# Sparsemax attention of a two-layer decoder: five loops written out, waits for constants moved to their instructions

## The chip, the cores and the metric

The kernel runs as one program on one core of a Trainium2 chip. The core has five engines with an instruction stream each: TensorE (PE, with its weight loads PEld), VectorE (DVE), ScalarE (ACT), GpSimd (POOL) and SyncE (SP), which here only starts transfers. They meet through semaphores: an instruction adds to one when it is done, and another instruction, or a separate waiting instruction in front of it, holds until the semaphore has reached a value. The metric is the device time of one execution in microseconds (us), the median of several runs.

## The reference

A decoder of two layers over 32 sequences of 100 rows of 256 numbers, in float32. Each layer has self attention, cross attention to a context of 361 rows, and a feed-forward block, each with a residual and a layer norm. The diff touches the cross attention of the second layer, whose weights come from a sparsemax in place of a softmax:

```python
def sparsemax(x):
    x = x - jnp.max(x, axis=-1, keepdims=True)
    zs = -jnp.sort(-x, axis=-1)
    rho = jnp.arange(1, L + 1, dtype=x.dtype)
    cssv = jnp.cumsum(zs, axis=-1) - 1.0
    support = zs > cssv / rho
    k = jnp.maximum(jnp.sum(support, axis=-1, keepdims=True), 1)
    tau = jnp.take_along_axis(cssv, k - 1, axis=-1) / k.astype(x.dtype)
    return jnp.clip(x - tau, 0.0)
scores = einsum('bhqd,bhkd->bhqk', qh, kh) * scale     # 16 heads of 16
out = einsum('bhqk,bhkd->bhqd', sparsemax(scores), vh) # then @ Wo + bo, residual, layer norm
```

## The kernel before

Seven stages follow each other, each with its own semaphores and tiles, whose names begin with the stage: `ta` (tanh attention), `ca` (cross attention), `ql` (quantised linear), `na` (normed attention), `sa` (the sparsemax attention), `me` and `ea` (experts), `cr` (collecting their rows). Between `sa` and `me` stands a second sparsemax stage `sb` behind a condition that these inputs do not meet, so it does not run. In each stage every engine has a program of its own; the order on each engine is the order in which its Python code calls the instructions, and nothing reorders it.

`sa` (`packed_sparse_attention`) handles one sequence at a time. Its 16 heads x 100 query rows are 1600 score rows, packed into 13 tiles of up to 128 rows x 361 keys, in two groups of 7 and 6 tiles. For a group the work runs around the engines. PE multiplies the scores (`scores`, L2747 and L2751), ACT copies them out of PSUM (`copy_scores`, L2882), and DVE takes the eight largest of each eighth of a row (`largest`, eight MAX8 at L3036 for each tile). From these candidates DVE and POOL work out a lower bound of the threshold: `bound` (L3052, L3055), then twice a `compare` on POOL (L2631) and a `refine` on DVE (L3065 to L3078, each instruction working on 6 or 7 columns that the one before it wrote), and L3085 to L3089 end it with `nt0`. With `nt0` ACT cuts the scores (`cut`, L2890), DVE counts what is left (`number`, L3098), DVE makes a Newton step (`update`, L3119 to L3130), ACT sums the excess (`excess`, `sign`, L2898 and L2906), DVE makes a second Newton step, and POOL subtracts the threshold (`probability`, L2641). PE turns the result (`turn`, L2765), ACT copies it (L2916), and PE multiplies by the values (`values`) and the output matrix.

The two groups are staggered, so that DVE goes through one sequence in two halves, each beginning with the `update` at L3119 and ending with the `nt0` at L3089 of the other group. Call half A the one that ends with group 0 of the next sequence (7 tiles), half B the one that ends with group 1 (6 tiles).

`passes` (L2595 to L2605) drives PE, ACT, DVE and POOL: `body` is written out for the first two sequences (m = 0), stands in a hardware loop for the next 28, two to a turn (`eng.Fori(1, B // 2 - 1)`, 14 turns), and is written out again for the last two and for what remains behind them. SP has a loop of its own (L2581, 13 turns). In a loop the values that semaphores are compared with come from a register that is worked out at run time; in the written-out parts they are constants.

`stand` (L91 to L96) is how several waits are put: a wait, and then an increment of a semaphore `turns` that nobody reads. The wait is carried by the increment, which is an instruction of its own in front of the one that needs the value. `Chain` uses it between DVE instructions that read each other's results, and between POOL's. Other waits are put with `wait_ge` alone, and then ride on the instruction that needs them, in the loop with a register's value as well as outside with a constant.

Of the kernel before, what the change touches and what calls it, by code (L numbers as in the profile page):

```python
# [26 lines left out]
B = 32  # L27
# [35 lines left out]
def open_all(eng, *events):  # L63

    for e in events:
        eng.sem_inc(e.sem, e.start)


class Chain:
# [15 lines left out]
    def wait(self):  # L85
        stand(self.eng, self.turns, self.sem, self.i * self.per + self.n)
# [5 lines left out]
def stand(eng, turns, sem, value):  # L92


    eng.wait_ge(sem, value)
    eng.sem_inc(turns, 1)  # L96


class Place:
# [53 lines left out]
def tanh_attention(nc, x, xT, Wq, bq, Wk, bk, Wv, bv, Wo, bo, out):  # L153
# [8 lines left out]
    with ExitStack() as ctx:  # L162
# [107 lines left out]
        def _(pool):  # L270
# [6 lines left out]
            with pool.Fori(0, G) as g:  # L277
                chain = Chain(pool, turns, pool_step, g, U * NORM_STEPS)

                def causal(u):  # L280

                    for r in range(4):
                        stand(pool, turns, *exp_done.at(g, 4 * u + r + 1))
                        heads = pT[:, u % 2, 4 * r:4 * r + 4, :]
                        pool.affine_select(out=heads, in_=heads, compare_op=ALU.is_ge, fill=0.0, base=0,  # L285
                                           pattern=[[0, 4], [1, S]], channel_multiplier=-1).then_inc(p_done.sem, 1)

                def norm(u):

                    pool.wait_ge(*stored[u % 2].at(g, u // 2))  # L290
                    stand(pool, turns, *mv_done.at(g, u + 1))
                    norm_rows(pool, chain, z[:, u % 2, :], mv[:, u % 2, :], rstd[:, u % 2, :], nbias[:, u % 2, :],
                              half[0:S, :], xn[:, u % 2, :], xn_done.sem)

                causal(0)
                causal(1)
                causal(2)
                norm(0)
                causal(3)
                norm(1)  # L300
                norm(2)
                norm(3)
                chain.end()
# [2064 lines left out]
def packed_sparse_attention(nc, x, cT, heads4, Wq, bq, Wk, bk, Wv, bv, WoS, bo, out, sum_max):  # L2368
# [20 lines left out]
    with ExitStack() as ctx:  # L2389
# [60 lines left out]
        turns = a.sem("turns")  # L2450
# [53 lines left out]
        def prev(m, u):  # L2504
            return (m, 0) if u else (m - 1, 1)
# [22 lines left out]
        @block.sync  # L2528
        def _(sp):
            open_all(sp, *xq_in, *cT_in, *xr_in, *stored)  # L2530
            sp.dma_start(wq[:, :, :], Wq.rearrange("(k p) n -> p k n", p=P)).then_inc(w_in, 16)
            sp.dma_start(wk[:, :, :], Wk.rearrange("(k p) n -> p k n", p=P)).then_inc(w_in, 16)
            sp.dma_start(wv[:, :, :], Wv.rearrange("(k p) n -> p k n", p=P)).then_inc(w_in, 16)
            sp.dma_start(wo[:, :, :], WoS.rearrange("(k p) n -> p k n", p=P)).then_inc(w_in, 16)
            sp.dma_start(bos[:, :], bo).then_inc(w_in, 16)
            sp.dma_start(bqs[:, :], bq).then_inc(w_in, 16)
            sp.dma_start(bks[:, :], bk).then_inc(w_in, 16)
            sp.dma_start(bvs[:, :], bv).then_inc(w_in, 16)
            sp.dma_start(hm[:, :], heads4).then_inc(w_in, 16)

            def load_x(m, u):
                n = 2 * m + u
                sp.wait_ge(*proj_done.at(n, -7))
                sp.dma_start(xq[:, u, :], x_s[n]).then_inc(xq_in[u].sem, 16)

            def load_c(m, u):
                n = 2 * m + u
                sp.wait_ge(*vp_done.at(n, -3))
                sp.dma_start(cTs[:, u, :, :], cT_s[n]).then_inc(cT_in[u].sem, 16)

            def load_residual(m, u):
                n = 2 * m + u
                sp.wait_ge(*xb_done.at(n, -1))
                sp.dma_start(xr[:, u, :], x_s[n]).then_inc(xr_in[u].sem, 16)

            def store(m, u):
                n = 2 * m + u
                sp.wait_ge(*xn_done.at(n, 1))
                sp.dma_start(out_s[n], xn[:, u, :]).then_inc(stored[u].sem, 16)

            def step(m, u, third=True, second=True, stores=True):

                if third:
                    load_x(m + 1 + u, 1 - u)
                if second:
                    load_c(m + 1, u)
                    load_residual(m + 1, u)
                if stores:
                    store(*prev(m, u))

            last = B // 2 - 1
            load_x(0, 0)
            load_c(0, 0)
            load_x(0, 1)
            load_c(0, 1)
            load_residual(0, 0)
            load_residual(0, 1)
            load_x(1, 0)
            step(0, 0, stores=False)
            step(0, 1)  # L2580
            with sp.Fori(1, last - 1) as m:  # L2581
                step(m, 0)
                step(m, 1)
            step(last - 1, 0)
            step(last - 1, 1, third=False)
            step(last, 0, third=False, second=False)
            step(last, 1, third=False, second=False)
            store(last, 1)
            sp.wait_ge(top_step, 1)
            sp.dma_start(sum_max, top[:, :]).then_inc(top_out, 16)  # L2590
            for u in range(2):
                sp.wait_ge(*stored[u].at(B // 2, 0))
            sp.wait_ge(top_out, 16)

        def passes(eng, body):  # L2595

            body(0, 0, behind=False)
            body(0, 1)
            with eng.Fori(1, B // 2 - 1) as m:
                body(m, 0)  # L2600
                body(m, 1)
            body(B // 2 - 1, 0, later=False)
            body(B // 2 - 1, 1, ahead=False, later=False)
            body(B // 2, 0, here=False, ahead=False, later=False)

        @block.gpsimd
        def _(pool):
# [75 lines left out]
            compare(0, 0, 0, 0)  # L2683
            compare(0, 0, 0, 1)
            passes(pool, sequence)

        @block.tensor
        def _(pe):
# [158 lines left out]
            for i in range(10):  # L2847
                scores(0, 0, i)
            passes(pe, sequence)

        @block.scalar
        def _(act):
# [56 lines left out]
            def copy_turned(m, u, q, t):  # L2909
                n = 2 * m + u  # L2910
                f = NK * q + t
                kn = KEYS[t][1]
                _, c0, cn = quad(q)
                act.wait_ge(*ov_done.at(n, 0))
                act.wait_ge(*tr_done.at(n, f + 1))
                act.activation(pT[0:kn, t, c0:c0 + cn], tr[f % 2][0:kn, 0:cn], ACT.Relu).then_inc(ca_done.sem, 1)  # L2916
# [85 lines left out]
            for i in range(7):  # L3002
                copy_scores(0, 0, i)
            passes(act, sequence)

        @block.vector
# [1105 lines left out]
```

## Time and profile before

| | |
|---|---|
| time, 3 runs | 4163.66 us median (4158.6 to 4169.7) |
| profiled execution, span | 4163.3 us, 83513 instructions |
| busy in the span | PE 3203.5 (77%), DVE 2250.9 (54%), ACT 2196.6 (53%), POOL 1452.4 (35%) |
| stage `sa` in the span | about 2130 to 3470 us |

The profile gives no separate time for the profiled execution; its span, first to last instruction, stands for it and lies 0.4 us under the median of the runs. Busy shares of the whole span mix seven stages with different limits, so the stage is read by itself. In a row of the timeline the two numbers ahead are the start and the duration in us, and a bracket at the end gives idle time of the engine in front of the instruction and what ended it, "issue" being time for which the profile shows no cause. Idle times of up to about 0.2 us get no bracket; they are the difference between a start and the end of the row before.

### The profile page before, as it was taken

The numbers are of one execution on the slowest core, as the hardware profiler recorded it, in microseconds if no ns is written. First come the engines' busy times: TensorE is split into PE (matmuls) and PEld (weight loads), VectorE is DVE, ScalarE is ACT, GpSimd is POOL, SyncE is SP. The second block draws the span as 40 slices with busy tenths as digits, with TensorE's granted clock in tenths as the row PEclk, the third lists the DMA queues.
The fourth block names the chain that finished last, engine by engine and source line by source line (L and its number), as shares of the span: only waits on it lengthen the run. The fifth ranks groups of instructions, "written<-read, shape, count | busy, mean of one in ns | idle before, by whom it ended". The sixth has DMA issues, their size and how long they took to land. (4 is left out here: it accounts for less than half of the span.)

```text
span 4163.3 us, 83513 instructions
## 1 busy us (share of the span) xinstructions
PE 3203.5 (77%) x21166; PEld 1978.6 (48%) x21166; DVE 2250.9 (54%) x10359; ACT 2196.6 (53%) x6653; POOL 1452.4 (35%) x2228
## 2 busy tenths in 40 slices
PE   7999998888888823888857777777777785687772
PEld 5666665566666622444424444444444444344441
DVE  1222222466666675666648888878887882211112
ACT  3433333466666601777738777777777782221110
POOL 1111111355555535555524444444443441110005
PEclk9999999899999966888858888887888775999996
DMA  1000000111111011000010000000000003206773
GB/s 61 20 12 12 14 14 10 56 37 38 36 37 35 26 38 48 21 22 22 21 39 15 18 17 17 20 16 18 16 18 16 18 8 128 77 31 207 225 228 110
DMA packets 111885, 189.45 MB, mean 46 GB/s; under 512 B 11150, under 2 KB 95886, under 8 KB 105550
## 3 DMA queue, kind: packets, MB, share of 16 engines
q1 hardware_dynamic: 102094, 166.32, 12.9%
q10 hardware_dynamic: 7200, 14.68, 0.9%
q0 software_dynamic: 2400, 6.56, 0.5%
q14 instruction: 151, 1.24, 0.1%
q8 instruction: 40, 0.66, 0.1%
HBM read 149.90 MB, written 37.62 MB: 45 GB/s over the span
## 5 line engine op out<-in xcount | busy, mean ns | idle before, releaser
L3036 DVE MAX8 sa_cand<-sa_s 128x8 f32<-128x45 f32 (+3 forms) x3328 | 405.6, 191 | 37.1 <-ACT sa_s L2882 30.9
L2765 PE MATMUL sa_tr<-sa_ident,sa_s 128*128 128x128 f32 (+3 forms) x1248 | 276.5, 339 | 187.5 <-POOL sa_s L2641 100.2
L852 ACT ACTIVATE ca_p<-ca_sm,ca_nb 100x361 f32<-100x361 f32 x512 | 301.9, 591 | 210.9 <-DVE ca_nb L936 209.9
L672 POOL TENSOR_SCALAR ca_p<-ca_p,ca_rec 100x361 f32<-100x361 f32 x512 | 286.8, 579 | 344.2 <-DVE ca_rec L950 343.9
L2641 POOL TENSOR_SCALAR sa_s<-sa_s,sa_unit,sa_nu 128x361 f32<-128x361 f32 (+1 forms) x416 | 261.4, 644 | 317.5 <-DVE sa_nu L3128 317.5
L2765 PEld LDWEIGHTS sa_tr<-sa_ident,sa_s 128*128 128x128 f32 (+3 forms) x1248 | 185.9, 179 | 284.9 <-issue 274.4
L2890 ACT ACTIVATE sa_s<-sa_s,sa_nt 128x361 f32<-128x361 f32 (+1 forms) x416 | 244.3, 592 | 94.1 <-DVE sa_nt L3089 94.1
L936 DVE CUSTOM_DVE_ANT_0 ca_sm<-ca_sc,ca_mb 100x361 f32<-100x361 f32 x512 | 252.3, 526 | 69.3 <-PE ca_sc L759 56.4
L2898 ACT ACTIVATE sa_spare_a<-sa_s,sa_nu 128x361 bf16<-128x361 f32 (+1 forms) x416 | 246.8, 594 | 69.5 <-DVE sa_nu L3130 69.3
L2631 POOL TENSOR_TENSOR sa_over<-sa_cand,sa_tc 128x280 f32<-128x280 f32 (+3 forms) x128 | 99.3, 776 | 453.2 <-DVE sa_tc L3055 277.6
L2751 PE MATMUL sa_sc<-sa_kT,sa_qm 32*128 32x361 f32 (+3 forms) x768 | 227.9, 522 | 20.5 <-ACT sa_s L2882 20.0
L2916 ACT ACTIVATE sa_pT<-sa_tr 128x512 f32<-128x512 f32 (+5 forms) x384 | 181.7, 497 | 103.6 <-PE sa_tr L2765 100.7
L770 PEld LDWEIGHTS ca_tr<-ca_ident,ca_p 100*128 100x128 f32 (+1 forms) x1536 | 171.9, 154 | 102.3 <-issue 73.5
L770 PE MATMUL ca_tr<-ca_ident,ca_p 100*128 100x100 f32 (+1 forms) x1536 | 208.8, 260 | 3.2 <-POOL ca_p L672 2.5
L3098 DVE TENSOR_SCALAR_CACHE_REDUCE sa_spare_d<-sa_s 128x361 bf16<-128x361 f32 (+1 forms) x416 | 202.9, 518 | 0.3 <-ACT sa_s L2890 0.3
L1628 ACT ACTIVATE na_p<-na_sm,na_nb 100x100 f32<-100x100 f32 x512 | 186.6, 370 | 22.3 <-DVE na_nb L1693 20.6
L2730 PE MATMUL sa_yo<-sa_wv,sa_cTs 128*128 128x256 f32 (+1 forms) x384 | 155.2, 544 | 50.8 <-DVE sa_vm L3025 50.7
L465 DVE TENSOR_TENSOR ta_vpre<-ta_proj,ta_bvs 100x512 f32<-100x512 f32 x64 | 44.3, 692 | 276.2 <-PE ta_proj L337 276.2
L2882 ACT ACTIVATE sa_s<-sa_sc 128x361 f32<-128x361 f32 (+1 forms) x416 | 178.1, 463 | 18.7 <-PE sa_sc L2751 14.2
L285 POOL TENSOR_SCALAR_AFFINE_SELECT ta_pT<-ta_pT 100x400 f32<-100x400 f32 x128 | 67.9, 542 | 318.6 <-ACT ta_pT L428 314.3
L1457 POOL TENSOR_TENSOR na_rs<-na_rs,na_half 100x32 f32<-100x32 f32 x32 | 174.5, 5453 | 2.7
L2751 PEld LDWEIGHTS sa_sc<-sa_kT,sa_qm 32*128 32x128 f32 (+3 forms) x768 | 83.1, 183 | 155.5 <-ACT sa_s L2882 92.6
(323 smaller groups left out, 7683.4 us busy)
## 6 DMA issues: line engine op xcount, KB each, us to landing
ea_we<-m_experts SPq DMA_DIRECT2D x40, 1024.0 KB, 6.4
ea_wd<-m_experts SPq DMA_DIRECT2D x40, 512.0 KB
ca_cTs<-cT SPq DMA_DIRECT2D x32, 361.0 KB
sa_cTs<-cT SPq DMA_DIRECT2D x32, 361.0 KB
rows_in<-me_zeros ACTq DMA_DIRECT2D x1, 7168.0 KB
ea_xe<-rows_in SPq DMA_DIRECT2D x40, 128.0 KB
rows_out<-ea_ye ACTq DMA_DIRECT2D x40, 128.0 KB
ca_ms<-mask SPq DMA_DIRECT2D x32, 141.0 KB
```

The lines of the kernel that those rows point to most:

```text
L672: ins = pool.tensor_scalar(p[:, r, j, :], p[:, r, j, :], rec[:, r, j:j + 1], 1.0, ALU.mult, ALU.mult)
L770: mm = pe.transpose(tr[f % 2][0:kn, j * S:(j + 1) * S], p[:, r, j, k0:k0 + kn], ident[0:S, 0:S])
L852: act.activation(p[:, r, j, :], sm[:, r % 2, j, :], ACT.Exp, bias=nb[:, r % 2, j:j + 1], scale=-1.0, accum_out=den[:, r, j:j + 1]).then_in ...
L936: dve.tensor_tensor_reduce(sm[:, r % 2, j, :], sc[j][0:S, 0:S2], mb[:, u, :], -1 / 4, 3e38, ALU.add, ALU.min, nb[:, r % 2, j:j + 1]).then_ ...
L1628: act.activation(p[:, r, j, :], sm[:, r, j, :], ACT.Exp, bias=nb[:, r, j:j + 1], scale=-1.0, accum_out=den[:, r, j:j + 1]).then_inc(exp_do ...
L2641: pool.tensor_scalar(s[0:rows, u, i, :], s[0:rows, u, i, :], unit[0:rows, :], nu2[0:rows, i:i + 1], ALU.mult, ALU.add).then_inc(p_done.sem, 1)
L2751: mm = pe.matmul(bank[0:rows, 0:S2], qm[hr, u, P * i:P * i + rows], kT[hr, u, i // 7, :], start=True, stop=True)
L2765: mm = pe.transpose(tr[f % 2][0:kn, c0:c0 + rows], s[0:rows, u, i, k0:k0 + kn], ident[0:rows, 0:rows])
L2890: act.activation(s[0:rows, u, i, :], s[0:rows, u, i, :], ACT.Relu, bias=nt0[0:rows, i:i + 1], accum_out=total[0:rows, i:i + 1]).then_inc(r ...
L2898: ins = act.activation(spare_a[0:rows, i, :], s[0:rows, u, i, :], ACT.Relu, bias=nu1[0:rows, i:i + 1], accum_out=total[0:rows, i:i + 1])
L3036: ins = dve.max(cand[0:rows, i, q, :], s[0:rows, u, i, PART[q]:PART[q + 1]])
L3098: ins = dve.tensor_scalar(spare_d[0:rows, i, :], s[0:rows, u, i, :], u1[0:rows, i:i + 1] if step else 0.0, 0.0, ALU.is_gt, ALU.add, accum_ ...
```

## The change

`stand` adds its increment only where the value is not a plain integer. Where it is one, the wait now rides on the next instruction of the engine. And the two loops of `sa`, in `passes` for four engines and in SP's program, become Python loops, so all 32 sequences are written out and every value in the stage is a constant.

```diff
     eng.wait_ge(sem, value)
-    eng.sem_inc(turns, 1)
+    if not isinstance(value, int):
+        eng.sem_inc(turns, 1)
@@ SP's program of packed_sparse_attention
-            with sp.Fori(1, last - 1) as m:
+            for m in range(1, last - 1):
                 step(m, 0)
                 step(m, 1)
@@ passes, for PE, ACT, DVE and POOL
-            with eng.Fori(1, B // 2 - 1) as m:
+            for m in range(1, B // 2 - 1):
                 body(m, 0)
                 body(m, 1)
```

Line numbers from 97 on are one higher after the change. The program of DVE in this stage goes from 1539 instructions (559 ahead of the loop, 591 in it, 389 behind it) to one run of 5907; those of PE from 1011 to 4232, of ACT from 547 to 2602, of POOL from 274 to 878. The order of the computing instructions on every engine is the same as before. The edit of `stand` touches the written-out parts of other stages too: outside `sa` and `sb`, 131 waits with a constant stood as instructions of their own on DVE and 114 on POOL, nearly all of which now ride on the instruction behind them.

On DVE, the end of the loop's second half A and the beginning of the next half B, before (instructions that only wait are not shown; REGISTER_ALU works out the value for one):

```order
L95 REGISTER_ALU
L3078 TENSOR_TENSOR sa_tc<-sa_tc,sa_shift 128x7
L95 REGISTER_ALU
L3085 TENSOR_SCALAR sa_low<-sa_tc 128x7
L3086 TENSOR_SCALAR sa_low<-sa_tc 128x7
L95 REGISTER_ALU
L3089 TENSOR_TENSOR sa_nt<-sa_low 128x7
L2599 REGISTER_ALU
L2599 COMPARE_AND_BRANCH
```

The same place on DVE after the change, the end of a half (here one with 6 columns) and the start of the next:

```order
L3079 TENSOR_TENSOR sa_tc<-sa_tc,sa_shift 128x6
L3086 TENSOR_SCALAR sa_low<-sa_tc 128x6
L3087 TENSOR_SCALAR sa_low<-sa_tc 128x6
L3090 TENSOR_TENSOR sa_nt<-sa_low 128x6
L3120 TENSOR_SCALAR sa_count<-sa_signs 128x4
L3121 RECIPROCAL sa_rec<-sa_count 128x7
L3037 MAX sa_cand<-sa_s 128x8 x4
```

The branch and the register work are gone, and the next half follows directly; the computing rows stand in the order in which they stood.

On POOL, in the loop before, the two `compare` of group 0 and what follows them:

```order
L95 ISA
L2631 TENSOR_TENSOR sa_over<-sa_cand,sa_tc 128x7x40
L95 REGISTER_ALU
L2631 TENSOR_TENSOR sa_over<-sa_cand,sa_tc 128x7x64
L2653 REGISTER_ALU
L143 TENSOR_SCALAR sa_rstd<-sa_mv 100x1
```

The same place on POOL after the change:

```order
L2632 TENSOR_TENSOR sa_over<-sa_cand,sa_tc 128x7x40
L2632 TENSOR_TENSOR sa_over<-sa_cand,sa_tc 128x7x64
L144 TENSOR_SCALAR sa_rstd<-sa_mv 100x1
```

Here too only the instructions between the computing ones went; each `compare` now carries its own wait for `tc`.

## Rows read from the trace of the kernel before

**Rows 1.** Busy time by engine, 28 sequences of the loop (window: length, then each engine).

```profile
2214.50:3363.00 1148.50, 893.12 (x5686) 515.41 (x5684) 950.18 (x5460) 897.97 (x2772) 472.31 (x700) 0.81 0.06 17
```

**Rows 2.** What DVE waited for, 2100 to 3500: us in total, times, longest.

```profile
DVE sa_count L3119 <- issue: 51.9, 14, 4.2
DVE sa_over L3065 <- POOL sa_over L2631: 51.4, 98, 1.1
...
DVE sa_cand L3036 <- issue: 3.6, 14, 0.3
...
DVE sa_spare_d L3098 <- ACT sa_s L2890: 0.3, 1, 0.3
```

**Rows 3.** Timeline of DVE: starts of halves in the loop and behind it.

```profile
2704.16 0.17 DVE L3119 TENSOR_SCALAR sa_count<-sa_signs 128x4 f32<-128x4 f32 x1
...
2727.98 0.17 DVE L3119 TENSOR_SCALAR sa_count<-sa_signs 128x4 f32<-128x4 f32 x1 [4.06 <-issue]
...
2747.50 0.17 DVE L3119 TENSOR_SCALAR sa_count<-sa_signs 128x4 f32<-128x4 f32 x1
...
2767.30 0.17 DVE L3119 TENSOR_SCALAR sa_count<-sa_signs 128x4 f32<-128x4 f32 x1
...
3363.15 0.17 DVE L3119 TENSOR_SCALAR sa_count<-sa_signs 128x4 f32<-128x4 f32 x1
...
3383.02 0.17 DVE L3119 TENSOR_SCALAR sa_count<-sa_signs 128x4 f32<-128x4 f32 x1
...
3402.21 0.17 DVE L3119 TENSOR_SCALAR sa_count<-sa_signs 128x4 f32<-128x4 f32 x1
...
3421.57 0.17 DVE L3119 TENSOR_SCALAR sa_count<-sa_signs 128x4 f32<-128x4 f32 x1
```

**Rows 4.** Groups by line, DVE: count | busy us, mean ns | idle before us.

```profile
L3069 DVE TENSOR_REDUCE sa_both<-sa_over 128x14 f32<-128x560 f32 (+3 forms) x128 | 109.7, 857 | 18.7
L3072 DVE RECIPROCAL sa_few<-sa_both 128x6 f32<-128x6 f32 (+1 forms) x128 | 25.3, 197 | 19.0 <-DVE sa_both L3069 0.5
L3120 DVE RECIPROCAL sa_rec<-sa_count 128x6 f32<-128x6 f32 (+1 forms) x128 | 25.2, 197 | 12.1 <-DVE sa_count L3119 2.3
L3075 DVE SCALAR_TENSOR_TENSOR sa_shift<-sa_both,sa_few 128x6 f32<-128x6 f32 (+1 forms) x128 | 24.9, 195 | 9.4
L3078 DVE TENSOR_TENSOR sa_tc<-sa_tc,sa_shift 128x6 f32<-128x6 f32 (+1 forms) x128 | 21.4, 167 | 18.8
L3142 DVE BATCH_NORM_STATS2 sa_stats<-sa_z 100x6 f32<-100x256 f32 x32 | 13.7, 427 | 1.1
L3085 DVE TENSOR_SCALAR sa_low<-sa_tc 128x7 f32<-128x7 f32 x64 | 11.0, 172 | 9.5
L3089 DVE TENSOR_TENSOR sa_nt<-sa_low 128x7 f32<-128x7 f32 x64 | 10.7, 167 | 12.4 <-DVE sa_low L3086 5.1
```

**Rows 5.** Timeline of DVE and POOL in one half A: DVE's `tc`, POOL's `compare`, DVE's answer.

```profile
2762.24 0.17 DVE L3078 TENSOR_TENSOR sa_tc<-sa_tc,sa_shift 128x7 f32<-128x7 f32 x1
...
2762.58 0.94 POOL L2631 TENSOR_TENSOR sa_over<-sa_cand,sa_tc 128x448 f32<-128x448 f32 x1 [2.97 <-DVE sa_tc L3078]
...
2763.55 0.43 DVE L3065 TENSOR_SCALAR sa_over<-sa_over 128x448 f32<-128x448 f32 x1 [0.65 <-POOL sa_over L2631]
```

**Rows 6.** Groups by line, POOL: a separate wait (L144) and one on its instruction (L1457).

```profile
L1457 POOL TENSOR_TENSOR na_rs<-na_rs,na_half 100x32 f32<-100x32 f32 x32 | 174.5, 5453 | 2.7
L144 POOL TENSOR_TENSOR sa_rstd<-sa_rstd,sa_half 100x1 f32<-100x1 f32 x32 | 18.3, 571 | 5.9 <-POOL sa_rstd L143 5.9
```

**Rows 7.** Timeline of ACT in one sequence: its four waits for DVE.

```profile
2756.42 0.59 ACT L2898 ACTIVATE sa_spare_a<-sa_s,sa_nu 128x361 bf16<-128x361 f32 x1 [1.60 <-DVE sa_nu L3130]
...
2767.39 0.60 ACT L2890 ACTIVATE sa_s<-sa_s,sa_nt 128x361 f32<-128x361 f32 x1 [1.53 <-DVE sa_nt L3089]
...
2776.45 0.60 ACT L2898 ACTIVATE sa_spare_a<-sa_s,sa_nu 128x361 bf16<-128x361 f32 x1 [1.18 <-DVE sa_nu L3130]
...
2786.70 0.60 ACT L2890 ACTIVATE sa_s<-sa_s,sa_nt 128x361 f32<-128x361 f32 x1 [1.88 <-DVE sa_nt L3089]
```

## The prediction

> **What bounds the stage now.** I read the busy shares by stage first, then what VectorE (DVE) waited for, then its timeline, and last the idle time in front of each of its lines. In the loop's 28 sequences DVE is busy 950.2 of 1148.5 us, more than PE (893.1) and ACT (898.0) [rows 1]. That alone proves little, since PE and ACT are close behind. The list of DVE's waits decides it: in the whole stage it waited 0.3 us for an ACT result inside the stream of tiles, and its two large rows name neither ACT nor PE [rows 2]. Its 198.3 idle us therefore have other owners. 51.9 us stand in front of L3119 with no cause shown, 51.4 us are waits for POOL's `compare` [rows 2], and the rest are short idle times in front of lines that read what DVE itself has just written [rows 4]. DVE sets the pace here: time that leaves its stream leaves the kernel, until another engine becomes late.
>
> **The loop's end.** A half A that runs into the loop's jump back takes 2727.98 - 2704.16 = 23.82 us; the next half A, inside the turn, takes 2767.30 - 2747.50 = 19.80 [rows 3]. The last half A of the loop, which leaves it without a jump, takes 3383.02 - 3363.15 = 19.87, with no pause in front of the L3119 that follows [rows 3]. So the pause belongs to the jump that is taken, 13 times in 14 turns: 13 x 4.02 = 52.3 us. Written out, DVE's code has no jump between the first sequence and the last. I take 52. During the pause the other engines drain and wait, so none of it comes back as somebody else's delay.
>
> **The waits between DVE's own instructions.** L3072 (a reciprocal behind a reduction) has 19.0 us of idle for 128, 148 ns each; L3069 and L3078 read the same, 146 and 147 [rows 4]. In front of each stands a separate waiting instruction. L3142 reads the row just written as well, but its wait rides on it: 1.1 us for 32, 34 ns each [rows 4]. L3120 has both kinds, 64 each, and its 12.1 us fit 64 x 147 + 64 x 34 ns = 11.6 [rows 4]. Exposed separate waits: L3069, L3072, L3075, L3078 and L3085 have 18.7 + 19.0 + 9.4 + 18.8 + 9.5 = 75.4 us; L3089 64 x 147 ns = 9.4 (the other 3.0 of its 12.4 belong to the loop's end, counted above); L3120 9.9; two lines outside the rows, L3052 and L3144, 32 waits each and priced like the others, 9.4. Together 104 us, or 22 waits for each of 32 sequences. Each now rides on its instruction: 104 x (1 - 34/147) = 80 us less. Bounds: 0, if the idle time belongs to the dependency and not to the extra instruction, and 104. I take 80, because the 34 ns stand in the same stream and between instructions of the same kind. Separate waits that are already met cost nothing I can see: the MAX8 behind them start without a gap.
>
> The Trainium skill, VectorE: DVE Perf Modes, section "The DRAIN you can't avoid", speaks against this term: it reports eight copies taking the same time with a semaphore on each as with one on the last, so that the semaphore costs nothing extra. By that rule this term would be 0 and the time that of rival 2 below. It measured increments, though; what goes here is an instruction that waits, and rows 4 price that at 113 ns.
>
> **POOL's answer.** Four times a sequence DVE hands `tc` to POOL and, after at most one other instruction, waits for `compare`; 98 of 128 waits show [rows 2], three a sequence. In one of them `tc` is done at 2762.24 + 0.17 = 2762.41, POOL starts at 2762.58, and DVE goes on 0.03 us after POOL ends [rows 5]. Of these 0.17 us the separate wait is some 0.10: POOL's L144 behind such a wait has 5.9 us for 32, 184 ns, and its L1457 with the wait riding on it 2.7 for 32, 84 ns [rows 6]. 98 x 0.10 = 9.8 us; bounds 0 and 98 x 0.17 = 16.7. I take 10.
>
> **Register work.** In the loop DVE also works out a register for nearly every wait. Behind the loop, in written-out code, half B takes 3402.21 - 3383.02 = 19.19 us against 2747.50 - 2727.98 = 19.52 inside, and half A 3421.57 - 3402.21 = 19.36 against 19.80 [rows 3]. That is at most 0.33 + 0.44 = 0.77 us a sequence, 28 x 0.77 = 21.6 us. It includes the loop's one pause a turn in front of L3036, 3.6 us in all [rows 2], and perhaps help from PE and ACT, which have less to do there. Bounds 0 and 21.6; I take 9, a little under the middle.
>
> **What rides elsewhere.** The 131 DVE and 114 POOL waits that change outside this stage would give 131 x 0.113 + 114 x 0.10 = 26 us if all were exposed, 0 if all hide. In those stages other engines set the pace for most of the time; I take 3.
>
> **What is late next.** ACT. In one undisturbed sequence, half A of 19.80 us [rows 3] and half B of 2786.70 - 2767.39 = 19.31 [rows 7], it waits for DVE 1.60, 1.53, 1.18 and 1.88 us [rows 7], 6.2 in all, so of 39.1 us it needs 32.9. DVE goes from the same 39.1 to about 39.1 - 22 x 0.113 - 0.3 for POOL - 0.3 for the registers = 36.0 us: still the longer. Phase by phase it is tight in one place: between the Newton step and `nt0` of half A, DVE loses 12 of the 22 waits and one POOL answer, 12 x 0.113 + 0.10 = 1.46 us, against 1.53 of slack. ACT then starts at once instead of waiting, which delays nobody as long as it catches up in the next phase, where it has 1.18.
>
> **Sum.** 52 + 80 + 10 + 9 + 3 = 154 us. The profiled execution spans 4163.3 us, 0.4 under the median of the runs; against that median the changed kernel takes 4163.7 - 154 = 4010 us.
>
> **Rivals.**
> 1. ACT or PE takes over. If half of what DVE gains outside the loop's end comes back as waits for ACT's cuts or PE's scores, 52 + 99 / 2 = 102 us are left: 4062. For it: ACT's slack is as small as 1.18 us [rows 7]. Against: DVE has waited 0.3 us for it in a stage where ACT's slack never vanished, and 32.9 stands against 36.0.
> 2. The 147 ns belong to the dependency, and a wait at its instruction costs as much. Then POOL's answer is unchanged as well, and 52 + 9 + 3 = 64 us are gained: 4100. Against it: L3142 and L1457 [rows 4, 6]. The Trainium skill's sentence above (VectorE: DVE Perf Modes) speaks for this one.
> 3. The straight code runs dry, and it is slower. 5907 instructions come past once where 591 came round; should fetching them pause DVE as the jump does, 4.0 us each time, then 154 / 4.0 = 38 pauses cancel the gain, one in 155 instructions, and 42 make it measurably slower (4180). The closing code, 389 instructions without a jump, and the opening code, 559, show no such pause: the 14 pauses at L3119 [rows 2] are 13 jumps and one at the loop's entry. By the 0.26 us pauses at L3036, one for 591 instructions, it would be 10 x 0.26 = 2.6 us, less than the 3.6 that go. The Trainium skill, Runtime: NRT & Kernel Launch, section "Instruction fetch mechanics", has code arrive in blocks of 256 instructions, with the crossing mostly hidden; as an estimate from that page, 5907 / 256 = 23 crossings, fewer than the 38 even if each cost a whole jump.
> 4. The change does not do what it says: the increments come back as other waiting instructions. The program has 236 of these left on DVE in this stage against 133 + 14 x 100 + 98 executed before, so this has next to no chance.
>
> **How the numbers follow.** The forecast's mechanism has 0.75, rival 1 0.11, rival 2 0.08, rival 3 0.06 in all: 0.03 for slower, 0.01 for no change, 0.02 for a smaller gain. Within 0.3% (12.5 us) a measurement of this kernel can't tell a difference from none. Faster 0.96, same 0.01, slower 0.03. The range goes down to 3990: POOL's answer at 16.7, register work at 21.6, and nothing else at its end, give 3991. Upwards it takes in rival 1 and most of the way to rival 2, to 4085; what lies above has about 0.1.
>
> **What would show it.** In the profile after, the pause at L3119 (now L3120) is gone and the halves lie 17.6 to 18.3 us apart throughout; the idle in front of the lines of rows 4 falls to about 4 us for 128; POOL starts `compare` 0.07 us after `tc`; ACT's waits for `nt0` shrink from 1.5 to 1.9 us to under 0.8. Wrong would be: the same 147 ns in front of L3073 (rival 2), DVE waiting for ACT or PE by more than 10 us in the stage (rival 1), or new pauses without a cause spread evenly over DVE or PE (rival 3).

## The result and the profile after

The changed kernel takes 3969.97 us, median of 4 runs (3966.1 to 3982.3), against 4166.51 (4158.6 to 4169.7) for the kernel before, run beside it: ratio 0.954, 95% interval 0.952 to 0.956. The forecast was 4010, its range 3990 to 4085. The direction was right, and what was forecast to go went; but the gain is 196 us by the medians and 193.1 by the two profiled spans (4163.3 and 3970.2), where 154 was forecast, and the time lies below the range.

The length of the stage can be read from one line: the distance between the first and the last start of the `update` instruction (L3119 before, L3120 after). Before it is 3454.0 - 2176.1 = 1277.9 us. The view of one line of the kernel after has count, duration in ns (least, median, most) and first and last start:

```profile
L3120 DVE TENSOR_SCALAR sa_count<-sa_signs x64: 167/170/171, 2162.8 to 3266.7; 128x4 f32<-128x4 f32 x64
```

That is 1103.9 us. So 174.0 of the 193.1 us come from the stage and 19.1 from outside it, 13.3 of these ahead of it (2176.1 to 2162.8). The 19.1 rest on one profile of each kernel, and the part outside the stage varies by more than 10 us between profiles of kernels that are alike there (shown with the other stages below). I use the length of the stage for every experiment below; it depends less than the whole time on what the other stages happen to do.

The busy times in the windows of the kernel after, for the 28 sequences that had been the loop (columns as in [rows 1]):

```profile
2198.00:3183.30 985.30, 812.01 (x5684) 481.50 (x5684) 926.05 (x5461) 886.59 (x2772) 473.20 (x700) 0.89 0.07 20
```

1148.5 us have become 985.3. DVE is now busy 94% of the time and still longest. PE needs 812.0 us where it needed 893.1 for the same number of matmuls: its granted clock rose from 0.81 to 0.89. So one of the two engines that rival 1 feared got faster as well.

Of the 163.2 us in this window, 139.1 are idle time of DVE (198.3 before, 59.3 after). The other 24.1 are busy time (950.2 before, 926.1 after) for the same instructions: more often now the next one starts while the one before is still running, and some run a little shorter. The clearest place is a MAX8 behind a reciprocal, before and after:

```profile
2747.82 0.20 DVE L3120 RECIPROCAL sa_rec<-sa_count 128x7 f32<-128x7 f32 x1
2748.06 0.53 DVE L3036 MAX8 sa_cand<-sa_s 128x8 f32<-128x45 f32 x4
```

```profile
2761.25 0.20 DVE L3121 RECIPROCAL sa_rec<-sa_count 128x7 f32<-128x7 f32 x1
2761.37 0.48 DVE L3037 MAX8 sa_cand<-sa_s 128x8 f32<-128x45 f32 x4
```

From start to start it was 0.24 us, without a gap that a bracket would show; now it is 0.12, and the two overlap by 0.08 us.

What DVE waited for in the kernel after (us in all, times, longest):

```profile
DVE sa_over L3066 <- POOL sa_over L2632: 41.6, 98, 1.0
...
DVE sa_count L3120 <- ACT sa_spare_a L2899: 5.7, 1, 5.7
...
DVE sa_count L3120 <- issue: 0.3, 1, 0.3
```

The 51.9 us in front of `update` are gone, and the wait for POOL fell from 51.4 to 41.6 [rows 2]. The single wait for ACT stands at the end of the stage. The halves in DVE's timeline now follow each other without a pause (start, duration):

```profile
2708.16 0.17 DVE L3120 TENSOR_SCALAR sa_count<-sa_signs 128x4 f32<-128x4 f32 x1
...
2725.88 0.17 DVE L3120 TENSOR_SCALAR sa_count<-sa_signs 128x4 f32<-128x4 f32 x1
...
2743.32 0.17 DVE L3120 TENSOR_SCALAR sa_count<-sa_signs 128x4 f32<-128x4 f32 x1
...
2761.05 0.17 DVE L3120 TENSOR_SCALAR sa_count<-sa_signs 128x4 f32<-128x4 f32 x1
```

17.72 us for half B, 17.44 for half A; [rows 3] had 19.52, 19.80 and 23.82. The prediction had said 17.6 to 18.3, so half A is shorter than forecast. The groups by line that answer to [rows 4]:

```profile
L3070 DVE TENSOR_REDUCE sa_both<-sa_over 128x14 f32<-128x560 f32 (+3 forms) x128 | 109.7, 857 | 4.4
L3073 DVE RECIPROCAL sa_few<-sa_both 128x6 f32<-128x6 f32 (+1 forms) x128 | 25.2, 197 | 4.4
L3121 DVE RECIPROCAL sa_rec<-sa_count 128x6 f32<-128x6 f32 (+1 forms) x128 | 25.2, 197 | 4.6 <-DVE sa_count L3120 0.2
L3079 DVE TENSOR_TENSOR sa_tc<-sa_tc,sa_shift 128x6 f32<-128x6 f32 (+1 forms) x128 | 21.4, 167 | 4.4
L3143 DVE BATCH_NORM_STATS2 sa_stats<-sa_z 100x6 f32<-100x256 f32 x32 | 13.7, 427 | 1.1
```

The last column is the one to read: 18.7 to 19.0 us for 128 have become 4.4, 34 ns each, the value that L3142 had before. The mean durations of these lines did not change. The 0.34 us between `tc` and POOL's start [rows 5] became 0.24 in the timeline after:

```profile
2774.29 0.17 DVE L3079 TENSOR_TENSOR sa_tc<-sa_tc,sa_shift 128x7 f32<-128x7 f32 x1
...
2774.53 0.94 POOL L2632 TENSOR_TENSOR sa_over<-sa_cand,sa_tc 128x448 f32<-128x448 f32 x1 [2.21 <-DVE sa_tc L3079]
...
2775.50 0.43 DVE L3066 TENSOR_SCALAR sa_over<-sa_over 128x448 f32<-128x448 f32 x1 [0.55 <-POOL sa_over L2632]
```

ACT's waits in one sequence: 0.70 and 0.70 us where [rows 7] had 1.88 and 1.60, and 1.25 where it had 1.18. The one in front of the first `cut` of the group of seven tiles, 1.53 before, is now too short for a bracket:

```profile
2761.17 0.60 ACT L2891 ACTIVATE sa_s<-sa_s,sa_nt 128x361 f32<-128x361 f32 x1 [0.70 <-DVE sa_nt L3090]
...
2769.33 0.59 ACT L2899 ACTIVATE sa_spare_a<-sa_s,sa_nu 128x361 bf16<-128x361 f32 x1 [0.70 <-DVE sa_nu L3131]
...
2787.28 0.60 ACT L2899 ACTIVATE sa_spare_a<-sa_s,sa_nu 128x361 bf16<-128x361 f32 x1 [1.25 <-DVE sa_nu L3131]
```

### The profile page after: what moved, and what is told of

Same layout as the page of the kernel before. It is cut to its first block and busy times, and to the rows that moved or that the text cites. A ratio compares the mean times of both kernels' runs of the same rounds, so it can differ in the third digit from the quotient of the medians.

```text
span 3970.2 us, 76439 instructions
## 1 busy us (share of the span) xinstructions
PE 3117.0 (79%) x21166; PEld 1942.5 (49%) x21166; DVE 2225.5 (56%) x10359; ACT 2184.4 (55%) x6653; POOL 1452.7 (37%) x2228
## 3 DMA queue, kind: packets, MB, share of 16 engines
q1 hardware_dynamic: 102094, 166.32, 13.3%
## 5 line engine op out<-in xcount | busy, mean ns | idle before, releaser
L2766 PE MATMUL sa_tr<-sa_ident,sa_s 128*128 128x128 f32 (+3 forms) x1248 | 231.1, 306 | 111.7 <-ACT sa_pT L2917 96.8
L937 DVE CUSTOM_DVE_ANT_0 ca_sm<-ca_sc,ca_mb 100x361 f32<-100x361 f32 x512 | 252.3, 526 | 69.7 <-PE ca_sc L760 65.9
L2899 ACT ACTIVATE sa_spare_a<-sa_s,sa_nu 128x361 bf16<-128x361 f32 (+1 forms) x416 | 247.3, 595 | 56.9 <-DVE sa_nu L3131 56.7
L2766 PEld LDWEIGHTS sa_tr<-sa_ident,sa_s 128*128 128x128 f32 (+3 forms) x1248 | 165.8, 161 | 180.8 <-ACT sa_pT L2917 126.1
```

The costliest lines, as they stand in the source:

```text
L937: dve.tensor_tensor_reduce(sm[:, r % 2, j, :], sc[j][0:S, 0:S2], mb[:, u, :], -1 / 4, 3e38, ALU.add, ALU.min, nb[:, r % 2, j:j + 1]).then_ ...
L2766: mm = pe.transpose(tr[f % 2][0:kn, c0:c0 + rows], s[0:rows, u, i, k0:k0 + kn], ident[0:rows, 0:rows])
L2899: ins = act.activation(spare_a[0:rows, i, :], s[0:rows, u, i, :], ACT.Relu, bias=nu1[0:rows, i:i + 1], accum_out=total[0:rows, i:i + 1])
```

## Experiments

Two groups of questions: which edit brings what (the first five), and where the 40 us more than forecast come from (the others). My theory was that two terms were too small: separate waits that are already met, which I had priced at nothing, would cost something behind a short instruction, and the other stages' waits were not hidden. The rivals to that are the prediction's own terms. "Separate again" below means that the named waits get their increment back, with everything else as in the changed kernel:

```diff
+def alone(eng, turns, sem, value):
+    eng.wait_ge(sem, value)
+    eng.sem_inc(turns, 1)
```

**One edit without the other.** First, `stand` alone, the loops kept (in the diff of the change, only the first part).

> Only the edit of stand; the two loops stay, so the 28 sequences inside keep their increments, and only the 4 written-out sequences and the other stages change. The prediction's terms: 4 x 22 x 0.113 = 10 us, POOL 1, elsewhere 3, together 14 us: ratio to before 0.9966. Rival (from the trace after the change: separate waits that are already met also cost something behind a short instruction, and the other stages gained about 19 us): 4 x 3.4 + 19 = 33 us, ratio 0.992. If the other stages' 19 us come from elsewhere than the waits, ratio 0.9966 too.

4127.6 us, ratio 0.992 (0.990 to 0.993), 36 us less. The stage is 16.7 us shorter. By the starts of the halves, 9.9 of these come from the written-out sequences (the three halves ahead of the loop and the four behind it take 118.9 us where they took 128.8), where 11 were forecast. Some 6.6 come from the loop, in which no DVE instruction was changed: the pause at its jump is 3.3 to 3.6 us here and not 3.9 to 4.2, as the wait list shows against [rows 2]:

```profile
DVE sa_count L3120 <- issue: 45.1, 14, 3.6
```

Why the same loop pauses for less behind a shorter opening is open. The span falls by 36.5 us, so 19.8 us come from outside the stage in these two profiles, as my theory had it.

Second, the loops alone, every increment kept.

> Only the loops written out; stand keeps its increment for every value. The prediction's terms: 52 for the loop's end and 9 for register work, 61 us, ratio 0.985. Rival: the register work is worth its upper bound, 0.77 us a sequence, 52 + 22 = 74 us, ratio 0.982. If straight code ran dry it would show pauses without a cause on DVE and a ratio above 0.99. Idle in front of the lines that read what DVE has just written stays at 146 to 148 ns each in all accounts.

4103.2 us, ratio 0.985 (0.984 to 0.987), 61 us less. That is the sum the prediction gave, but partly by luck: the stage is 1209.3 us long, 68.6 shorter, and what lies outside it came out 7 us longer in this profile than in that of the kernel before. The 68.6 are the 51.9 of the pauses and 16.7 of what the prediction calls register work. The groups by line show the separate waits at their old price, 154 ns each here:

```profile
L3072 DVE RECIPROCAL sa_few<-sa_both 128x6 f32<-128x6 f32 (+1 forms) x128 | 25.2, 197 | 19.7 <-DVE sa_both L3069 1.5
```

The timeline of DVE in this kernel shows something new. Most halves take 19.15 to 19.20 us, but some take 0.3 more:

```profile
3007.27 0.17 DVE L3119 TENSOR_SCALAR sa_count<-sa_signs 128x4 f32<-128x4 f32 x1
...
3026.45 0.17 DVE L3119 TENSOR_SCALAR sa_count<-sa_signs 128x4 f32<-128x4 f32 x1
...
3045.96 0.17 DVE L3119 TENSOR_SCALAR sa_count<-sa_signs 128x4 f32<-128x4 f32 x1
...
3065.51 0.17 DVE L3119 TENSOR_SCALAR sa_count<-sa_signs 128x4 f32<-128x4 f32 x1
```

19.18, 19.51, 19.55. 23 of 58 halves are late by more than 0.1 us, about 7 us in all; in the changed kernel it is 2 of 59, 0.7 us. These irregular delays have no owner in the profile. They look like a mild form of rival 3, but that they are instruction fetch I have not shown. They are not chance, though: in the next run, which has the same DVE program in the stage, the same 23 halves are late.

**Whose jump.** In the kernel before, only DVE's loop is written out, or only those of the other engines (there SP's too); increments stay.

```diff
-            with eng.Fori(1, B // 2 - 1) as m:
-                body(m, 0)
-                body(m, 1)
+            if loop:
+                with eng.Fori(1, B // 2 - 1) as m:
+                    body(m, 0)
+                    body(m, 1)
+            else:
+                for m in range(1, B // 2 - 1):
+                    body(m, 0)
+                    body(m, 1)
```

> The kernel before with DVE's loop alone written out; PE, ACT, POOL and SP keep theirs, and every increment stays. If the jump that counts is DVE's: as much as with all loops written out, 69 us in the stage, ratio to before 0.984. Rival: the other engines jump too and their slack is only 1.2 to 1.9 us a half; if their jumps take 4 us as well and were hidden only behind DVE's, then 2 to 3 us a turn come back, 13 x 2.5 = 32 us, ratio 0.991, with DVE waiting for ACT or PE once a turn.

> The kernel before with the loops of PE, ACT, POOL and SP written out; DVE keeps its own, and every increment stays. If the jump and the register work that count are DVE's: ratio to before 0.999 to 1.000, the pauses in front of L3119 still 13 x 4.0 us. Rival: the others' jumps are part of the pause: up to 20 us less, ratio 0.995.

DVE's loop alone: 4095.9 us, ratio 0.984 (0.981 to 0.986), stage 1209.4 us, the same as with all loops written out (1209.3). The others' loops alone: 4169.7 us, ratio 1.002 (1.000 to 1.003), stage 1278.9. What DVE waited for in that kernel:

```profile
DVE sa_count L3124 <- issue: 51.7, 14, 4.1
```

The pause and the register work are DVE's own. The other engines jump too, but what that costs them is hidden even when DVE no longer jumps. With the increments in place, writing out the other four loops brought nothing. POOL's has a use all the same: `stand` drops the increment only for a constant, so the 9 to 13 us of POOL's waits below need POOL's loop written out too.

**A jump for four sequences instead of two.** On PE, ACT, DVE and POOL, in the kernel before.

```diff
-            with eng.Fori(1, B // 2 - 1) as m:
-                body(m, 0)
-                body(m, 1)
+            with eng.Fori(0, (B // 2 - 2) // 2) as k:
+                for m in (2 * k + 1, 2 * k + 2):
+                    body(m, 0)
+                    body(m, 1)
```

> The kernel before with four sequences to a turn instead of two (7 turns, 6 jumps in place of 13) on PE, ACT, DVE and POOL; increments and registers stay. If the pause is paid once for each jump taken: 7 x 4.02 = 28 us less, ratio 0.993. If it grows with the code that comes round again: 0, ratio 1.000, with 6 pauses of about 8 us.

4129.2 us, ratio 0.992 (0.990 to 0.994). The wait list names 21.1 us in front of L3120, 7 times, where 51.9 stood [rows 2]; six of them are jumps of 3.1 to 4.0 us, as this one in the timeline:

```profile
2706.39 0.17 DVE L3120 TENSOR_SCALAR sa_count<-sa_signs 128x4 f32<-128x4 f32 x1 [3.99 <-issue]
```

The pause is paid per jump and does not grow with a body twice as long. The stage is 36.4 us shorter; 30.8 of these are the pauses, and 1.8 the short pause in front of the MAX8, 3.6 us before [rows 2] and 1.8, 7 times, here. The remaining 3.8 I have not assigned. All register instructions are still there, so not all of what the loop costs beside its jumps is register work.

**The exposed waits.** The six waits of `refine` separate again (20 a sequence).

> The changed kernel, but the six chain waits of each refine step on DVE are separate instructions again (20 a sequence, 640 in all, of which 18 a sequence stand behind the instruction whose result they wait for, and 2 behind a copy, where they are met already). The prediction: 18 x 32 x 0.113 = 65 us over the changed kernel, near 4035, ratio to before 0.969. If the time belongs to the dependency and not to the separate instruction: 0, 3970, ratio 0.953. If the met waits cost about 0.1 us too: 65 + 6 = 71 us, ratio 0.970.

4036.2 us, ratio 0.971 (0.969 to 0.974), 66 us over the changed kernel. The stage is 1168.6 us, 64.7 more; forecast was 65. In the groups by line the reciprocal behind the reduction has its 148 ns back, while the one in `update`, whose wait was left riding, keeps 36 ns:

```profile
L3079 DVE RECIPROCAL sa_few<-sa_both 128x6 f32<-128x6 f32 (+1 forms) x128 | 25.2, 197 | 19.0 <-DVE sa_both L3076 0.5
L3127 DVE RECIPROCAL sa_rec<-sa_count 128x6 f32<-128x6 f32 (+1 forms) x128 | 25.2, 197 | 4.6 <-DVE sa_count L3126 0.2
```

Same dependency, same instruction, and the time follows the separate instruction. Rival 2 is refuted.

**The waits that are met already.** In front of the MAX8 groups, first the three right behind a reciprocal, then the other ten; the condition of the second is the reverse.

```diff
-                    stand(dve, turns, *z_in.at(n, pos + 1))
+                    (alone if pos in (0, 7, 11) else stand)(dve, turns, *z_in.at(n, pos + 1))
```

> The changed kernel, but in front of three of the thirteen MAX8 groups of a sequence, those right behind a reciprocal of 0.17 us, the wait for ACT's copy is a separate instruction again (96 in all, already met). The prediction's view, that met waits cost nothing: 0, ratio to before 0.953. Rival: a separate instruction behind a short one keeps the next from starting while the short one ends, 0.09 to 0.14 us each: 96 x 0.12 = 11 us, ratio 0.9555, and the MAX8 start 0.1 us later behind the reciprocal.

> The changed kernel, but the wait in front of the other ten MAX8 groups of a sequence, which stand behind longer work or behind other MAX8, is a separate instruction again (320 in all, already met). The prediction's view: 0, ratio to before 0.953. Rival that only short neighbours matter: 0 to 3 us as well. Rival that every instruction taken costs its own time whatever stands in front: 320 x 0.11 = 35 us, ratio 0.961.

Behind a reciprocal: 3976.2 us, ratio 0.955 (0.953 to 0.957); the stage is 1106.5 us, 2.6 more. The others: 3966.0 us, ratio 0.954 (0.952 to 0.955), stage 1103.8, nothing. Then the rest of DVE's waits in the stage, those of `bound`, `update` and `output`, separate again. These are 16 a sequence (the expectation counts 14): four exposed, twelve met.

> The changed kernel with the remaining DVE waits of this stage (in bound, update and output: 14 a sequence, 448 in all) as separate instructions again; refine and the MAX8 keep theirs at the instruction. Four a sequence stand exposed behind the instruction whose result they read. The prediction: 4 x 32 x 0.113 = 14 us over the changed kernel, the other ten nothing; stage length from the first to the last L3119 near 1118 us. Rival: the met ones cost 0.03 to 0.06 us each as well (the runs so far leave 17 us of the stage unassigned): 14 + 10 x 32 x 0.05 = 30 us, stage 1134.

3996.6 us, ratio 0.960 (0.958 to 0.962). The stage is 1120.4 us, 16.5 more: the four exposed ones at their 0.11 us, and 2.5 for the twelve, about what irregular delays make in this kernel (8 or 9 of 59 halves late, 2 us). So my theory on the met waits fell: for constants the prediction's sentence that they cost nothing holds, but for the 2.6 us behind a reciprocal.

**POOL's answer.** The wait of `compare` separate again.

> The changed kernel, but POOL's wait in front of each compare is a separate instruction again (128). The prediction's term: 98 waits of DVE longer by 0.10 us each: 10 us, ratio to before 0.9555; DVE's waits for compare go from 41.6 back to 51.4 us. Rival that POOL's wait costs the same either way: 0, ratio 0.953.

3980.6 us, ratio 0.956 (0.955 to 0.958). DVE's wait list has the old number to the tenth [rows 2], and the stage is 1113.0 us, 9.1 more:

```profile
DVE sa_over L3072 <- POOL sa_over L2638: 51.4, 98, 1.1
```

**All together.** With groups put back one by one, 93 us of the 105.4 between the loops-only kernel (1209.3) and the changed one (1103.9) were accounted for: 64.7 + 16.5 + 2.6 + 9.1. So all of DVE's waits in the stage separate again, and all of POOL's.

> The changed kernel with every DVE wait of this kind in the stage as a separate instruction again; POOL's and the other stages' stay at their instructions. If the groups add up: 64.7 + 16.5 + 2.6 = 84 us, the stage 1188 us from first to last L3119, time near 4054. If they cost more together than alone: up to 105.4 - 9.1 = 96 us, stage 1200, time near 4066.

> The changed kernel with every POOL wait of this kind in the stage as a separate instruction again (compare, probability, the layer norm, the heads' mask). If only the compare counts, as the prediction has it: 9 us, stage 1113, time near 3980. If the missing 12 us are POOL's: 21 us, stage 1125, time near 3992.

DVE's: 4065.9 us, ratio 0.978 (0.975 to 0.980). POOL's: 3984.0 us, ratio 0.957 (0.954 to 0.960). The line of `update` in the one and in the other:

```profile
L3133 DVE TENSOR_SCALAR sa_count<-sa_signs x64: 169/170/171, 2166.5 to 3356.4; 128x4 f32<-128x4 f32 x64
```

```profile
L3133 DVE TENSOR_SCALAR sa_count<-sa_signs x64: 154/169/170, 2163.8 to 3280.3; 128x4 f32<-128x4 f32 x64
```

1189.9 us is 86.0 over the changed kernel, 2 more than the groups' sum; the groups add up. 1116.5 is 12.6 over it, 3.5 more than `compare` alone. 105.4 - 86.0 - 12.6 = 6.8 us appear in neither. They may come where DVE's and POOL's waits are separate at once, or belong to the waits that `stand` puts on PE, which no run put back by themselves.

The windows from the first to the last `update` split these gains into idle and busy time of DVE (its busy time is the third behind the length; length less busy is idle). In order: the kernel before, the loops alone, all of DVE's waits, all of POOL's, and the changed kernel:

```profile
2176.10:3454.00 1277.90, 993.06 (x6337) 572.66 (x6334) 1056.30 (x6070) 1003.12 (x3099) 524.18 (x780) 0.81 0.06 16
2178.70:3388.00 1209.30, 972.33 (x6337) 561.06 (x6334) 1044.43 (x6070) 999.11 (x3099) 524.17 (x780) 0.83 0.06 18
2166.50:3356.40 1189.90, 975.79 (x6337) 565.02 (x6334) 1037.92 (x6069) 998.70 (x3099) 525.12 (x780) 0.83 0.06 18
2163.80:3280.30 1116.50, 905.15 (x6338) 533.62 (x6337) 1033.90 (x6069) 993.56 (x3100) 524.38 (x780) 0.89 0.07 19
2162.80:3266.70 1103.90, 907.97 (x6338) 537.26 (x6337) 1030.95 (x6070) 991.62 (x3100) 525.14 (x780) 0.88 0.07 19
```

In idle time the loops brought 56.7 us (51.9 of them the pauses), DVE's waits 79.0 and POOL's 9.7; the prediction had 80 and 10 for the last two. In busy time they brought 11.9, 7.0 and 2.9 more. In all, idle time fell by 148.7 us and busy time by 25.3.

**The other stages.** Outside the stage every such wait separate again.

> The changed kernel, but outside this attention stage every wait of this kind is a separate instruction again, as before. The prediction's term: 3 us over the changed kernel, ratio to before 0.954. Rival: the 19 us that the other stages gained in the profile are these waits: 3989, ratio 0.958, with quantised linear about 4.7, normed attention about 5.5 and the collecting of rows about 5 us longer than in the changed kernel. If those 19 us have another cause (where the code lies, transfers), the stages keep their new lengths.

3985.7 us, ratio 0.958 (0.956 to 0.959); the stage is unchanged at 1104.0 us. By the medians 16 us come back, by the spans 13.8. Other runs agree: the span less the stage is 2870 to 2893 us in the six kernels whose waits outside the stage are separate (mean 2880.3) and 2860 to 2874 in nine whose waits ride there (mean 2866.3), 14.0 less. So the 19.1 of the two profiles and the 19.8 above hold some 5 us of chance. Most of it is in two places. From the last `ca` instruction on DVE's L936 to the first `na` instruction at L1693 (as numbered before), quantised linear between them, it is 195.0 us here, 194.3 before and 189.3 after. The last stage, collecting rows, is the clearer one: POOL there does nearly everything itself. Groups by line of POOL in that stage, first with separate waits, then in the changed kernel:

```profile
L3958 POOL DMA_INDIRECT cr_yg<-rows_out,cr_index x25 | 25.4, 1017 | 10.3 <-issue 6.1 <-POOL cr_index L3955 4.2
...
L3971 POOL TENSOR_SCALAR cr_nbias<-cr_nbias 128x5 f32<-128x5 f32 x5 | 5.7, 1143 | 1.1 <-POOL cr_nbias L3970 1.1
```

```profile
L3945 POOL DMA_INDIRECT cr_yg<-rows_out,cr_index x25 | 24.7, 989 | 7.8 <-issue 6.1 <-POOL cr_index L3942 1.7
...
L3958 POOL TENSOR_SCALAR cr_nbias<-cr_nbias 128x5 f32<-128x5 f32 x5 | 2.5, 502 | 0.5
```

The idle columns of all lines of this stage on POOL add up to 15.0 and 10.1 us, and the stage is 71.7 and 66.8 us long from its first gather on. `na` does not follow its waits: its length from first to last L1693 was 428.5 us with them separate, 431.4 after and 436.9 before, so the 5.5 us there are not this term.

**A faster version.** The changed kernel with the loops of the other stages that run written out too (`with X.Fori(a, b) as m` becomes `for m in range(a, b)`, 26 places). This also turns the waits in these loops into constants, so `stand` drops their increments; the run does not separate the two.

> The changed kernel with the loops of all other stages that run written out as well. If a taken jump costs the pace-setting engine of cross attention and normed attention what it cost DVE here (4.0 us), 14 + 13 jumps give up to 108 us: ratio to before 0.928. If jumps are hidden there (PE and ACT wait for others anyway): 0 to 20 us, ratio 0.949 to 0.953. If the longer code must be fetched while the stages are short, it is slower than the changed kernel.

3921.8 us, ratio 0.943 (0.941 to 0.944), 48 us faster than the changed kernel, between the bounds. The stage is the same 1103.9 us. The largest part is cross attention, from the first to the last L937: 703.4 us became 671.7. Windows over that stage, in the changed kernel and in this one:

```profile
755.00:1460.00 705.00, 628.56 (x6585) 431.04 (x6582) 454.43 (x1709) 438.12 (x1335) 359.42 (x690) 0.96 0.12 35
```

```profile
765.00:1438.00 673.00, 607.61 (x6585) 416.51 (x6578) 460.84 (x1708) 438.45 (x1333) 357.07 (x689) 1.00 0.13 38
```

PE, the busiest there, lost 11 us of idle time and 21 us of busy time; its granted clock went from 0.96 to 1.00, which is 2.4 GHz throughout. 31.7 us for 14 jumps is 2.3 us each, less than the pause on DVE. That this is because another engine sets the pace there is likely, but not shown.

## Why the prediction was wrong

| term | forecast, us | measured, us | from |
|---|---|---|---|
| loop's end | 52 | 52 | pauses gone with DVE's loop |
| register work | 9 | 17 | loops alone: 68.6 - 51.9; not registers alone |
| DVE's separate waits | 80 | 86 | all of DVE's put back |
| POOL's answer | 10 | 13 | all of POOL's put back; `compare` 9 |
| left in the stage | - | 7 | 105.4 less the two rows above |
| elsewhere | 3 | 14 to 19 | put back: 14 by spans, 16 by medians; 19 outside the stage in the two profiles |
| sum | 154 | 189 to 194 | spans: 193.1 |

One row is a remainder, and the upper value of another is one too, so that the sum closes is no proof of its parts.

- **Two steps failed.** The first is **"What rides elsewhere ... I take 3"**: it measured 14 to 19, that is 11 to 16 of the 39 us between forecast and measured gain. It was argued from which engine sets the pace "for most of the time", without reading the two stages where DVE and POOL work alone one instruction after another. There the 0.1 us are exposed, as a row of the kernel before shows, in the view by line over the last stage; 10.3 us of idle time here became 7.8:

```profile
L3944 POOL DMA_INDIRECT cr_yg<-rows_out,cr_index x25 | 25.4, 1017 | 10.3 <-issue 6.1 <-POOL cr_index L3941 4.2
```

- **The second is the pricing of the stage by DVE's idle time alone.** In the stage 151 us were forecast and 174.0 measured. Idle time fell by 148.7, close to the forecast; the 25.3 us by which busy time fell are in no term, except where register work took its size from whole halves. Seen by term, the miss in the stage is the 8, 6, 3 and 7 us of the table. The prediction's "the MAX8 behind them start without a gap" shows the step: there was no gap, but behind a reciprocal there was an overlap to win, 0.12 us in the rows above.
- **The loop's end** was right in place, size and owner: 13 jumps of about 4.0 us, and DVE's alone.
- **The waits between DVE's instructions** were right in mechanism and price: 34 ns instead of 147, 64.7 us for `refine` where the same arithmetic gave 65, and 79.0 us of idle time for all of them where 80 was forecast. The 86 of the table has 7 us of busy time in it.
- **POOL's answer** was right for `compare` to a microsecond. POOL's other separate waits in the stage add 3.5, which the term left out.
- **Register work** is nearer the upper bound (21.6) than the value taken. The closing halves in [rows 3] had shown 0.77 us a sequence; I halved it for fear that PE and ACT had helped there. In the steady halves of the loops-only kernel it is 39.1 - 38.3 = 0.8 us, all of it DVE's; the irregular delays took some back. That registers are the whole cause is not shown: four sequences to a turn gave 5.6 us beside the pauses at L3120 with every register instruction kept.
- With elsewhere at 14 to 19 and the register work at 17, the forecast would have been 3986 to 3991, at the lower end of the range and still above the measured 3970; the rest is what DVE's and POOL's waits brought above their terms and the 7 us left over.
- **Rival 1** did not happen: DVE waited 0.2 us for an ACT result inside the stream, and PE became faster. **Rival 2** is refuted by the `refine` run. **Rival 3** happened in a small form, if these delays are fetches: not in the changed kernel (0.7 us) but where straight code also carries the separate instructions (about 7 and 5 us). **Rival 4** did not happen.

## What to carry to other kernels

In this stage, an instruction that only waits, behind the instruction it waits for, cost about 0.11 us on DVE and 0.10 on POOL more than a wait that rides; a met one cost almost nothing, so count the exposed ones. Look at busy time as well as at idle time: what stands between two instructions can also keep them from overlapping, and no idle column shows that. Ask for every stage, also the short ones, which engine works alone there: small costs that the long stages hide are paid in full in serial ones. The loop's jump cost DVE, which sets the pace, 3.1 to 4.2 us a turn and no more with a body twice as long, so write out that engine's loop first, or put more work into a turn. No run let the waits ride inside the loop, with a register's value, as other waits here do; that might bring their part without writing anything out.

## What was unexpected

- The clock that PE was granted in the stage rose from 0.81 to 0.89 when DVE's pauses went, and in cross attention from 0.96 to 1.00 with the loops written out there; its busy time fell with it. In the stage most of the rise goes with DVE's waits: by the windows above it is 0.81 before, 0.83 with the loops written out, 0.83 in the changed kernel with DVE's waits separate, 0.89 with POOL's separate, and 0.88 with all riding.
- Straight code was late irregularly, about 0.3 us at a time: in 23 of 58 halves with the increments in all programs, 20 of 59 with DVE's increments alone, 11 with those of `refine`, and 2 with none. The more separate instructions stand in DVE's program, the more of these delays there are. They come at the same places again where DVE's program in the stage is the same.
- Writing out the loops of four engines that do not set the pace, with the increments kept, gained nothing and may have cost a little (ratio 1.000 to 1.003).
